# GNN layer pair on one core: the adjacency stage's block loop in five forms by block range

## What is computed

```python
h = relu(layernorm(x))
# layer 0: gcn_conv twice (128 -> 64 -> 128); out[d] = sum over edges (s, d) of (h @ W)[s] * dinv[s] * dinv[d], plus self loop
x = x + gcn(relu(gcn(h, W1, b1)), W2, b2)
h = relu(layernorm(x))
# layer 1: per edge w = silu(edge_attr @ We1 + be1) @ We2 + be2
agg = segment_sum(w * (h[src] @ Wlin), dst)
x = x + h + silu(agg @ Wn1 + bn1) @ Wn2 + bn2
```

| blocks (8 windows each) | tiles that a window touches |
|---|---|
| 0 to 2 | 9 to 79 |
| 3 to 8 | 5 to 9 (two windows with 9) |
| 9 to 16 | 4 to 6 |
| 17 to 24 | 3 to 5 |
| 25 to 48 | 3 or 4, but for the last two windows of block 48 (2 and 6) |

## Time and profile before

### The profile page before, as it was taken

How to read it: one execution, slowest core, us unless ns; L and a number is a source line. 1 busy time by engine, 2 the same in 40 slices (tenths; PEclk the granted TensorE clock), 3 DMA queues, 4 the chain that set the end, 5 groups by cost and what they waited for, 6 DMA issues and landing times.

```text
span 3494.4 us, 70143 instructions
## 1 busy us (share of the span) xinstructions
PE 2937.5 (84%) x19624; PEld 2134.7 (61%) x19625; DVE 2056.2 (59%) x4694; ACT 959.5 (27%) x2055; POOL 1497.0 (43%) x1601
## 2 busy tenths in 40 slices
PE   5979999999999879977777878788778777887877
PEld 4742456777677679955555556556555555555555
DVE  7999999999998844443443344334434443443343
ACT  5110224455566511122212112222122222222212
POOL 0000000000000000067777777777777777777774
PEclk8989999999999989978888887887887888888788
DMA  2000011222223379733333333333333333333332
GB/s 62 0 0 0 38 56 75 84 92 104 112 112 130 138 289 347 285 75 78 79 78 80 80 77 80 80 76 79 79 80 77 80 80 80 79 77 79 77 77 69
DMA packets 278856, 324.79 MB, mean 93 GB/s; under 512 B 231023, under 2 KB 238344, under 8 KB 266142
## 3 DMA queue, kind: packets, MB, share of 16 engines
q1 hardware_dynamic: 227518, 217.13, 18.7%
q0 software_dynamic: 51168, 106.07, 11.5%
HBM read 238.00 MB, written 85.09 MB: 92 GB/s over the span
## 4 chain that ended last, share of the span: by engine, by line
POOL 41%; PE 34%; issue 17%; DVE 5%; DVEq 1%; ACT 1%; POOLq 1%; DMA 0%; ACTq 0%; SPq 0%
POOL shared L504 41%; PE pb L1318 8%; PE pa L1318 8%; PE pc L1312 6%; PE pd L1312 5%; PE pd L1276 3%; PE pf L1278 1%; DVE shared L960 1%; PE pb L1419 1%; DVE loop L960 1%; ACT shared L642 1%; DVEq L960 0%; PE pa L1412 0%; PE pb L1546 0%; PE pb L1286 0%
## 5 line engine op out<-in xcount | busy, mean ns | idle before, releaser
L504 POOL DMA_INDIRECT shared<-lin_table,idx x1568 | 1482.1, 945 | 479.1 <-issue 477.6
L1139 DVE TENSOR_TENSOR shared<-pb,shared 128x512 f32<-128x512 f32 x392 | 252.5, 686 | 1174.2 <-DMA shared<-lin_table,idx 1174.2
L533 POOL DMA_DIRECT2D lin_table<-c x12 | 9.3, 771 | 1476.1 <-issue 1286.5
L1493 PE MATMUL pb<-we_sb,shared 128*128 128x128 f32 x3136 | 629.5, 363 | 0.0
L1493 PEld LDWEIGHTS pb<-we_sb,shared 128*128 128x128 f32 x3136 | 535.0, 258 | 122.8 <-issue 122.5
L736 ACT ACTIVATE shared<-pa,be_col 128x512 f32<-128x512 f32 x392 | 248.2, 684 | 1110.6 <-PE pa L1482 1110.6
L1489 PE MATMUL pb<-be_parts,ones 3*128 3x512 bf16 x392 | 181.5, 463 | 400.4 <-DVE shared L1139 400.2
L960 DVE TENSOR_SCALAR shared<-col_h,shared 128x784 bf16<-128x784 f16 x1027 | 383.0, 416 | 5.4 <-issue 4.3
L1489 PEld LDWEIGHTS pb<-be_parts,ones 3*128 3x128 bf16 x392 | 36.6, 93 | 465.0 <-issue 449.6
L1482 PE MATMUL pa<-shared,we_sb 64*128 64x512 f32 x784 | 298.0, 847 | 0.7 <-ACT shared L731 0.7
L1318 PE MATMUL pb<-shared,c 128*128 128x392 bf16 x1376 | 278.8, 331 | 1.9 <-DVE shared L960 0.7
(11 more groups left out here) (233 smaller groups left out, 3731.4 us busy)
## 6 DMA issues: line engine op xcount, KB each, us to landing
adjacency<-shared SPq DMA_DIRECT2D x49, 1568.0 KB, 5.6
shared<-adjacency SPq DMA_DIRECT2D x49, 1568.0 KB, 8.7
shared<-in_edge_attr_dram SPq DMA_DIRECT2D x195, 256.0 KB, 3.1
shared<-lin_table,idx POOLq DMA_INDIRECT x1568
lin_table<-c POOLq DMA_DIRECT2D x12, 256.0 KB, 7.1
out_dram<-xr SPq DMA_DIRECT2D x12, 256.0 KB
shared<-in_dst_dram SPq DMA_DIRECT2D x1, 512.0 KB
shared<-in_src_dram SPq DMA_DIRECT2D x1, 512.0 KB
```

Source lines behind the costliest of these rows:

```text
L504: pool.indirect_dma_start(out=dest(s, j), out_offset=None, in_=table, in_offset=bass.IndirectOffsetOnAxis(ap=idx[:, s, j:j + 1], axis=0)). ...
L1139: dve.tensor_tensor(msgs[s % 2][:, h, :, :], pb[:, h, :].rearrange("p (i f) -> p i f", f=F), rows[:, h, :, :], ALU.mult).then_inc(msg_read ...
L1493: last = pe.matmul(pb[:, h, i * F:(i + 1) * F], act_t[:, h, i * P:(i + 1) * P], we2_sb[:, :], start=False, stop=(i == 3))
```

## The change

The two ranges of blocks become five, each with a form of the code for a window. A form is (first block, head, `more`): with `more` = None a window is built as before; with 2 it has a pair outside any branch, then a counted loop of pairs; with 1 a single outside any branch, then a counted loop of singles; with 0 a counted loop of singles alone. The counted loops of these forms have no `If_lt` around them, on either engine. The first unit takes buffer `w % 2`, all that the loop makes take `1 - w % 2`. `windows` is written in ten instructions in place of four, its ends less the head and `more`.

```diff
+FORMS = ((0, HEAD, None), (3, HEAD, 2), (9, HEAD, 1), (17, HEAD, 0), (SHORT, SHORT_HEAD, 0))
+FORM_ENDS = [first for first, _, _ in FORMS[1:]] + [NB]
...
-                for blocks, head in ((slice(0, SHORT), HEAD), (slice(SHORT, NB), SHORT_HEAD)):
+                for (first, head, more), end in zip(FORMS, FORM_ENDS):
+                    blocks, sure = slice(first, end), head + (more or 0)
...
-            def build_block(b, i, k, first=False, short=False):
-                head = SHORT_HEAD if short else HEAD
+            def build_block(b, i, k, form, first=False):
+                _, head, more = form
+                short, sure = head == SHORT_HEAD, head + (more or 0)
...
-                    with dve.If_lt(spans[w], spans[WB + w]):
-                        if short:
-                            single(w % 2, first_tile, head)
-                            dve.reg_add(start, spans[w], 1)
-                        else:
+                    if more == 2:
+                        loop_pair(w % 2, first_tile, head)
+                    if more == 1:
+                        single(w % 2, first_tile, head)
+                    if more is None:
+                        with dve.If_lt(spans[w], spans[WB + w]):
                             odd_pair(dve, lead, start, spans[w], spans[WB + w])
                             with dve.If_ne(lead, 0):
                                 loop_pair(w % 2, first_tile, head)
...
+                    else:
+                        last_tile = dve.snap(spans[WB + w], min_val=0, max_val=UNITS - sure)
+                        with dve.Fori(first_tile, last_tile, T if more == 2 else 1) as u:
+                            if more == 2:
+                                loop_pair(1 - w % 2, u, sure)
+                            else:
+                                single(1 - w % 2, u, sure)
                     head_columns(1)
...
-            build_block(0, 0, 0, first=True)
-            for turns, short in (((0, SHORT // 2), False), ((SHORT // 2, NB // 2), True)):
-                with nc.Fori(*turns, engines=bass.OrderedEngineSet([dve.engine]), hint_back_edge=True) as it:
-                    build_block(it * 2 + 1, 1, it, short=short)
-                    build_block(it * 2 + 2, 0, it + 1, short=short)
+            build_block(0, 0, 0, FORMS[0], first=True)
+            for form, end in zip(FORMS, FORM_ENDS):
+                with nc.Fori(form[0] // 2, end // 2, engines=bass.OrderedEngineSet([dve.engine]), hint_back_edge=True) as it:
+                    build_block(it * 2 + 1, 1, it, form)
+                    build_block(it * 2 + 2, 0, it + 1, form)
```

More of the change, by code:

```diff
@@ L57 @@
 assert SHORT % 2 == 1 and SHORT_HEAD == T + 1
+FORM_ENDS = [first for first, _, _ in FORMS[1:]] + [NB]
+assert all(end % 2 for end in FORM_ENDS)
 def gnn_kernel(nc, x, src, dst, edge_attr, W1, b1, W2, b2, We1, be1, We2, be2, Wlin, Wn1, bn1, Wn2, bn2, out):
@@ L860, in _ @@
                 of = span_ps[n].rearrange("a (b w) -> a b w", w=WB)
-                for blocks, head in ((slice(0, SHORT), HEAD), (slice(SHORT, NB), SHORT_HEAD)):
+                for (first, head, more), end in zip(FORMS, FORM_ENDS):
+                    blocks, sure = slice(first, end), head + (more or 0)
                     to = windows[:, blocks, n, :]
                     if n == 0:
-                        dve.tensor_scalar(to, of[:, blocks, :], float(UNITS - head), None, ALU.min).then_inc(windows_ready, 1)
+                        dve.tensor_scalar(to, of[:, blocks, :], float(UNITS - sure), None, ALU.min).then_inc(windows_ready, 1)
                     else:
-                        dve.tensor_scalar(to, of[:, blocks, :], -float(head), 0.0, ALU.add, ALU.max).then_inc(windows_ready, 1)
+                        dve.tensor_scalar(to, of[:, blocks, :], -float(sure), 0.0, ALU.add, ALU.max).then_inc(windows_ready, 1)
             dve.wait_ge(w_loaded, 16 * (N_W - 3))
@@ L949, in _ @@
             lead, start = dve.alloc_register("lead_dve"), dve.alloc_register("start_dve")
-            dve.wait_ge(windows_ready, 4)
+            dve.wait_ge(windows_ready, 2 * len(FORMS))
             for t in range(HEAD):
@@ L974, in build_block @@
                 for w in range(WB):
-                    first_tile = dve.snap(spans[w], min_val=0, max_val=UNITS - head)
+                    first_tile = dve.snap(spans[w], min_val=0, max_val=UNITS - sure)
                     def head_columns(j):
@@ L988, in build_block @@
                         for o in range(2):
-                            if short:
+                            if more is not None:
                                 dve.wait_ge(tile_hot[o][0], units[o])
@@ L1016, in build_block @@
                                 loop_pair(w % 2, first_tile, head)
[L1017 to L1021, removed]
+                            with dve.If_lt(start, spans[WB + w]):
+                                with dve.Fori(dve.snap(start, min_val=0, max_val=UNITS - sure),
+                                              dve.snap(spans[WB + w], min_val=1, max_val=UNITS - sure), 2 * T) as u:
+                                    loop_pair(1 - w % 2, u, head)
+                                    loop_pair(w % 2, u, head + T)
+                    else:
[5 more added lines that the diff above has]
+                                single(1 - w % 2, u, sure)
                     head_columns(1)
@@ L1260, in _ @@
             pe.wait_ge(w_loaded, 16 * (N_W - 3))
-            pe.wait_ge(windows_ready, 4)
+            pe.wait_ge(windows_ready, 2 * len(FORMS))
             pe.sem_inc(hist_used, RING - 1)
@@ L1330, in head_counts, with build_block @@
                 return last.then_inc(head_used[j], 1)
-            def build_block(b, i, first=False, short=False):
+            def build_block(b, i, form, first=False):
+                _, head, more = form
+                short = head == SHORT_HEAD
                 window_spans(pe, ranges, b)
@@ L1350, in single @@
                         pe.sem_inc(tile_used[e][1], 1)
[L1352 to L1356, removed]
+                    if more == 2:
+                        loop_pair(w % 2)
+                    if more == 1:
+                        single(w % 2)
+                    if more is None:
+                        with pe.If_lt(ranges[w], ranges[WB + w]):
                             odd_pair(pe, lead, start, ranges[w], ranges[WB + w])
@@ L1359, in build_block @@
                                 loop_pair(w % 2)
-                        with pe.If_lt(start, ranges[WB + w]):
-                            with pe.Fori(start, ranges[WB + w], 2 * T):
+                            with pe.If_lt(start, ranges[WB + w]):
+                                with pe.Fori(start, ranges[WB + w], 2 * T):
+                                    loop_pair(1 - w % 2)
+                                    loop_pair(w % 2)
+                    else:
+                        with pe.Fori(ranges[w], ranges[WB + w], T if more == 2 else 1):
+                            if more == 2:
                                 loop_pair(1 - w % 2)
-                                loop_pair(w % 2)
+                            else:
+                                single(1 - w % 2)
                     head_counts(ps, b, w, 1, short)
@@ L1370, in _ @@
             pe.wait_ge(deg_ready, 2)
-            build_block(0, 0, first=True)
+            build_block(0, 0, FORMS[0], first=True)
             pe.wait_ge(split_ready[0], 2)
[L1373 to L1376, removed]
+            for form, end in zip(FORMS, FORM_ENDS):
+                with nc.Fori(form[0] // 2, end // 2, engines=bass.OrderedEngineSet([pe.engine]), hint_back_edge=True) as it:
+                    build_block(it * 2 + 1, 1, form)
+                    build_block(it * 2 + 2, 0, form)
             pe.wait_ge(win_out, NW + 2)
```

## The result

The changed kernel takes 3613.9 us (median of 4 runs, 3612.2 to 3615.9) where the kernel before takes 3497.1 (median of 4 runs): a ratio of 1.033, 95% interval 1.032 to 1.035. It is slower, by 117 us; the forecast was 3618. The runs of one kernel lie within 0.2% of each other; the median of the kernel before was 3495.1 when the forecast was made, with three runs, and is 3497.1 with the fourth.

The account below looks back on a forecast made before the run. Bound: the stage lies on the path with VectorE and TensorE nearly full, VectorE the larger after the change. Added need 115.9 plus exits 6.6 gave 122.5 on 3496.07, 3618.6; the median lies 1.0 lower, so 3618, range 3587 to 3648.

Parts of the forecast that it names:

- The work of empty loop bodies: Blocks 3 to 48: unguarded loop bodies run at least once, adding 247 tiles and 286 units; bound rises 115.9 us.
- The rest over the need: Stage time above the larger engine need, 37.5 us; without the 3.3 us stall, 34.2 us was kept unchanged.
- It stays as it is: The `window_spans` register load, 1.103 us of VectorE's sequencer per block, 0.47 showing ahead of window 5, was taken as unchanged.
- the first rival: Branches were on the path: all of today's gaps vanish, stage 845.8 us, +78.4, so 3574; 13% for 3574 to 3600.
- Branches at 0: Fewer compares per window on VectorE, 0.116 us each, were taken to gain 0, with bounds 0 and 34.2 us.
- The exits: Leaving loops with prefetched back edges behind blocks 8 and 16 stalls VectorE, 2 x 3.3 = 6.6 us added.
- Behind the stage: All later stages stay as before, only later; a change of more than some us there would be a wrong sign.
- A loop that tests first: Rival: counted loops with nothing to do skip their body, 36 tiles less and 24 units more, -7.3, so 3488; 3%.
- Branches on the path: The same as the first rival: gaps vanish, exits included, +78.4, so 3574; 13%.
- engines that disturb each other more: Second rival: VectorE and TensorE wait in turn, all 61.6 us VectorE leaves today stays, +146.6, so 3642; 18%.
- the change does nothing: Rival: the added tiles hide in VectorE's slack in the stage, put at 20 of 332 us in blocks 25 to 48; 1%.

Follow-up runs that it names:

- e1_guard: The changed kernel with the branch put back around each counted loop of the new forms, on both engines: 3487.4 us, 0.9979 of the kernel before.
- e6_guard_work: e2_late with a branch around each counted loop of blocks 25 to 48 and one tile beyond the head in each window there: 1.0109 of the kernel before.
- e4_late_work: The kernel before, its window table changed so each window of blocks 25 to 48 has at least one tile beyond its head: 3560.3 us, 1.0186.
- e2_late: The changed kernel with only two ranges: blocks 0 to 24 built as before, 25 to 48 in the new form without a branch: 3541.0 us, 1.0135.
- e3_ranges: The kernel before with its block loop cut into the same five ranges, windows built exactly as before: 3524.4 us, 1.0088 of the kernel before.
- e5_align: The changed kernel with VectorE's loop over blocks 9 to 16 placed at the start of a 256-slot page: 1.0239 of the kernel before.
- the first four experiments: e1_guard, e2_late, e3_ranges and e4_late_work, run on one chip where the kernel before takes 3494.6 us: 3487.4, 3541.0, 3524.4 and 3560.3 us.

## Why the prediction was right

**The work of empty loop bodies** was the step that decided, and it held to the instruction: 247 tiles and 286 units more. Its price held too. Blocks 3 to 8 took 166.2 us where the sum gave 165.9 of need; blocks 26 to 47 took 15.42 a block where their instructions' pitch gives 15.04. Against the kernel that keeps the guards (`e1_guard`), the stage is 127 us longer, of which the empty work is 123.

**The rest over the need** was kept at 34.2 us, to which exits added: 37.5 + 6.6 = 44.1. Measured, the stage is 879.1 - 845.8 = 33.3 over VectorE's need, 11 less; this is where the forecast of the stage (889.9) was high. Two errors offset each other in it. Stalls take some 21 us, not 9.9: 6.0 at back edges, and some 15 at the starts of blocks 9, 17 and 25, taking each block against the later ones of its range. That leaves some 12 us where 34.2 were kept. "It stays as it is" was wrong: the 0.47 us ahead of window 5 shrink to 0.19 in block 29, though the load still takes 1.10 us, and VectorE's waits for nothing shown fall from 25.3 to 4.1 us in blocks 25 to 48. `e6_guard_work` against `e4_late_work` shows that code which stays loaded is worth 0.76 us a block at equal work. The sum had this rule only as a reading of the exits, worth 6.6 us. So the mechanism of the first rival, gaps that vanish, was in part true; the stalls and what came behind the stage kept the time from falling towards its 3574 to 3601.

**Branches at 0** was close: 0.25 us a block (`e6_guard_work` against `e2_late`) where the loop is short and VectorE is the bound, some 6 us in blocks 25 to 48. The change dropped that branch, but at the price of the surplus work.

**The exits** were sized at 3.3 us each, for two, with gaps of that size behind blocks 8, 16 and 24. `e3_ranges` says 4 for each start of a range on average, and the trace of the change has VectorE's stalls at 4.28, 2.24 and 2.04 us. It isn't VectorE's exit alone: TensorE stalls too (3.47 us in block 17), with nothing shown that it waited for. That this is the first pass through new code is likely, but no run tested it. The three back-edge stalls of blocks 11 to 15, 6.0 us, were not foreseen; they come from where that loop lies (`e5_align`).

**Behind the stage** nothing was expected. The span from ScalarE's last copy of the stage to the end is 2285.8 us before and 2293.4 after, 7.6 more. On the same kind of chip it was 2291.0, 2287.6, 2282.9 and 2284.5 for the first four experiments, whose code behind the stage is the same and only lies elsewhere. These differ among themselves by 8 us, so the 7.6 may be no more than that spread. Whether place is the cause was not tried; it stays open. This 7.6 hid most of the 11 us by which the stage was forecast too long. That the forecast came within 4 us is therefore luck; the sound part is the 115.9 us of added need, which the stage's 111.7 nearly equals. The forecast had named a change of more than some us behind the stage as a sign of being wrong, and there is one.

**The rivals.** A loop that tests first is ruled out by the counts, and 3488 was a fair price for what it would have done: `e1_guard`, which is that kernel but for the branch, has 3487.4. Branches on the path and engines that disturb each other more were both outside the result. On "the change does nothing" the forecast misread its row: by busy time VectorE has 332.2 - 300.0 = 32 us of slack in blocks 25 to 48, not 20, which is still less than half of the 69.5 added.

## What to carry to other kernels

Before a guard around a counted loop is dropped, find out whether the loop's body runs when its count is zero, and count on the real data how often it is: here the surplus body cost VectorE 0.54 us a window, the branch 0.03 on average. When engine needs are within a few per cent of each other, work out each one's need from pitches and take the larger by stage; that gave the added time of the stage to 4 us of 112, while what was kept on top of it was off by 11. In blocks 25 to 48, a loop body small enough to stay in VectorE's instruction memory was worth three times the branch in it, 0.76 against 0.25 us a block, and the number of instruction packets in the profile tells at once whether it does.

## What was not expected of the hardware

- A loop of VectorE that executes some 434 instructions a turn stalls 1.8 to 2.1 us at each back edge, although that edge carries a prefetch hint, and has no such stall when moved to the start of a page (`e5_align`). In `e3_ranges` the place of one loop decided 22 us of 3524, with about one packet of code more in each turn.
- At equal instructions, fetching the body again in each turn costs VectorE 0.76 us a block of 15.7 (`e4_late_work`, `e6_guard_work`), with 55 packets against none.
- A new range can stall TensorE as well: 3.47 us in block 17 of the changed kernel, 3.54 and 5.81 in blocks 9 and 17 of `e3_ranges`. The cause was not tested.
